# Gate products of an mLSTM layer with the tokens as stationary operand, summed on VectorE and turned back by TensorE

## The reference

```python
h_in = _rmsnorm(x, norm1_w)
q = (h_in @ wq) ; k = (h_in @ wk) ; v = (h_in @ wv)      # 128, 128, 256 columns
o_pre = h_in @ w_og                                      # 256 columns
i_pre = cap(h_in @ w_ig + b_ig)                          # 8 columns, cap(x) = 15 tanh(x / 15)
f_pre = cap(h_in @ w_fg + b_fg)                          # 8 columns
logfg = log_sigmoid(f_pre) ; Fcum = cumsum(logfg)        # along the tokens
Dmat = Fcum[s] - Fcum[t] + i_pre[t], causal ; m = max over t
C = (q k^T / 4) * exp(Dmat - m) ; n = max(|sum C|, exp(-m)) ; h = (C / n) v
```

## Time and profile before

| | |
|---|---|
| median of three executions | 673.02 us |
| profiled execution, its own time | 672.34 us |
| its span, first to last instruction | 670.6 us |
| granted TensorE clock, mean over the span | 0.995 |
| TensorE busy | 658.1 us (98%) |
| VectorE busy | 438.3 us (65%) |
| ScalarE busy | 411.3 us (61%) |
| GpSimd busy | 246.7 us (37%) |

### The profile page before, as it was taken

The page is one execution under the profiler, slowest core; times in us unless marked ns, Lnnn a source line. Parts: engine busy times, 40 slices in busy tenths (PEclk is TensorE's granted clock), DMA queues, the critical chain, the costliest instruction groups (busy, mean ns, idle before and its releaser), DMA issues. The chain is left out here.

```text
span 670.6 us, 15275 instructions
## 1 busy us (share of the span) xinstructions
PE 658.1 (98%) x5297; PEld 633.0 (94%) x5297; DVE 438.3 (65%) x968; ACT 411.3 (61%) x1085; POOL 246.7 (37%) x279
## 2 busy tenths in 40 slices
PE   8999999999999999999999999999999999999995
PEld 8999999999999999999999899999987799999995
DVE  6556557557666655765665576556569986556877
ACT  5556677666776666866577773334689864333553
POOL 3731972134353133632328555112451462222011
PEclk9999999999999999999999999999999899999999
DMA  7174654435534436534363404000166100000000
GB/s 254 37 219 160 193 172 140 133 101 174 168 127 113 127 108 185 161 128 126 97 183 124 111 1 151 32 0 2 48 208 243 65 1 1 1 1 0 1 33 31
DMA packets 38172, 69.74 MB, mean 104 GB/s; under 512 B 3440, under 2 KB 22640, under 8 KB 37872
## 3 DMA queue, kind: packets, MB, share of 16 engines
q1 hardware_dynamic: 37696, 68.38, 32.8%
q10 hardware_dynamic: 432, 0.79, 0.4%
HBM read 52.18 MB, written 16.97 MB: 103 GB/s over the span
## 5 line engine op out<-in xcount | busy, mean ns | idle before, releaser
L312 PE MATMUL PJ<-xTh,WBh 128*128 128x256 f32 x364 | 106.7, 293 | 0.3 <-POOL WBl L839 0.3
L314 PE MATMUL PJ<-xTh,WBl 128*128 128x256 f32 x364 | 103.0, 283 | 0.0
L313 PE MATMUL PJ<-xTl,WBh 128*128 128x256 f32 x364 | 102.8, 283 | 0.0
L824 POOL TENSOR_TENSOR stage<-stage 128x256 f32<-128x256 f32 x32 | 24.5, 766 | 165.0 <-DVE stage L691 165.0
L584 ACT ACTIVATE probs<-probs,rinv 128x256 f32<-128x256 f32 x128 | 58.4, 507 | 26.7 <-DVE rinv L707 26.7
L1202 PE MATMUL UG<-xTh,WBh 128*128 (+1 forms) x256 | 73.6, 288 | 0.3 <-PEq L54 0.3
L1205 PE MATMUL UG<-xTh,WBl 128*128 (+1 forms) x256 | 72.4, 283 | 0.0
L1203 PE MATMUL UG<-xTl,WBh 128*128 (+1 forms) x256 | 72.4, 283 | 0.0
L1274 ACT ACTIVATE ga<-UG 128x256 f32<-128x256 f32 x64 | 24.5, 383 | 75.1 <-PE UG L1205 75.1
L312 PEld LDWEIGHTS PJ<-xTh,WBh 128*128 128x128 f32 x364 | 69.6, 191 | 0.9 <-issue 0.5
L313 PEld LDWEIGHTS PJ<-xTl,WBh 128*128 128x128 f32 x364 | 69.6, 191 | 0.0
(11 more groups left out here) (320 smaller groups left out, 2385.9 us busy)
## 6 DMA issues: line engine op xcount, KB each, us to landing
K<-scr_k SPq DMA_DIRECT2D x60, 256.0 KB, 4.3
raw<-in_w_att SPq DMA_DIRECT2D x37, 256.0 KB, 4.7
Q<-scr_q SPq DMA_DIRECT2D x15, 512.0 KB, 7.5
stage<-scr_m SPq DMA_DIRECT2D x6, 768.0 KB, 5.9
scr_q<-rot_h SPq DMA_DIRECT2D x30, 128.0 KB
scr_q<-rot_l SPq DMA_DIRECT2D x30, 128.0 KB
scr_k<-rot_h SPq DMA_DIRECT2D x30, 128.0 KB
scr_k<-rot_l SPq DMA_DIRECT2D x30, 128.0 KB
```

What stands on the lines that cost most here:

```text
L312: pe.matmul(out, ah, bh, start=(i == 0), stop=False)
L313: pe.matmul(out, ah, bl, start=False, stop=False)
L314: last = pe.matmul(out, al, bh, start=False, stop=(i == n - 1))
L824: pool.tensor_tensor(y[:, 0:S], c[:, 0:S], sn[:, S:2 * S], ALU.subtract).then_inc(rope_sum, 1)
```

## The change

The gate products turn round: 128 tokens are stationary (a tile of `xh_v` or `xl_v`), and 32 weight columns move (8 heads x 2 gates x high and low part). A token tile of a batch takes 4 matmuls, a batch 8, all batches 32. High and low part of the weights give separate columns in OUTS; VectorE adds the pairs with two reduce instructions (`add_gates`) and writes the sums into `gt` with tokens on partitions; TensorE turns them back with 4 transposes into X (`gates_T`); then the Tanh reads X for both gates. `gt` is set to zero at the layer's start. The gates of batches 0, 1 and 2 stand together behind project(0); those of batch 3 come behind q and k of batch 1; `gates_T` stands between the two halves of v and output gate of batch 1. The gate weights are stored without padding. ScalarE's order changes too: it runs `gates` in two parts with half of `evac_og(1)` between them, and the MLP's weight pieces 5 to 11 stand at other places between the evacuations.

```diff
-        WGh, WGl = (gate_w[:, i * 2 * KT * WIDE:(i + 1) * 2 * KT * WIDE].rearrange("p (t g n) -> p t g n", t=KT, g=2)
-                    for i in range(2))
+        WG = WI[:, 11, PIECE - KT * 2 * GATES:].rearrange("p (t l n) -> p t l n", t=KT, l=2)
+        WG_part = [WG[:, :, l, :].rearrange("p t (g h) -> p t g h", g=2) for l in range(2)]
...
-        gate_sums = (X[:, 0:S], OUTS[:, 1, 0:S])
+        gate_parts = OUTS[:, 1, 0:B * TT * 2 * GATES]
+        gate_tok = gt[:, :, :].rearrange("p a s -> p (a s)").rearrange("p (t g k) -> p t g k", t=TT, g=2)
+        gate_sums = (X[:, 0:S], X[:, S:2 * S])
...
-                w = slice(96 - 32 * c, 96 - 32 * c + P)
-                for n, out in enumerate(gate_sums):
-                    for i in range(3 * KT):
-                        t, (a, b) = i // 3, ((WGh, xh_v), (WGh, xl_v), (WGl, xh_v))[i % 3]
-                        last = pe.matmul(out, a[:, t, n, w], b[:, t, c, :], start=(c == 0 and i == 0),
-                                         stop=(c == B - 1 and i == 3 * KT - 1))
-                last.then_inc(s_["gates_ready"], 1)
+                for t in range(TT):
+                    rows, at = slice(t * P, (t + 1) * P), (TT * c + t) * 2 * GATES
+                    for i in range(2 * KT):
+                        last = pe.matmul(gate_parts[:, at:at + 2 * GATES], (xh_v, xl_v)[i % 2][:, i // 2, c, rows],
+                                         WG[:, i // 2, :, :], start=(i == 0), stop=(i == 2 * KT - 1))
+                if c == B - 1:
+                    last.then_inc(s_["gates_ready"], 1)
+
+            def gates_T():
+
+                pe.wait_ge(s_["gates_added"], 2)
+                for n in range(2):
+                    for t in range(TT):
+                        last = pe.transpose(gate_sums[n][:, t * P:(t + 1) * P], gate_tok[:, t, n, :], ident[:, :])
+                last.then_inc(s_["gates_ready"], 1)
...
             project(0)
-            for c in range(B - 2):
+            for c in range(B - 1):
                 project_gates(c)
             pe_T(pe, 1, B - 1)
-            project_gates(B - 2)
-            project_qk(1)
+            project_part(1, 0)
+            project_part(1, 1)
             project_gates(B - 1)
-            project_vog(1)
+            project_vog(1, 0)
+            gates_T()
+            project_vog(1, 1)
             project(2)
...
+            act_hi(act, 1, 3)
             evac_og(0)
-            act_hi(act, 1, 3)
-            mlp_hi(5, 6)
             evac_q(1)
-            mlp_hi(6, 7)
             evac_k(1)
+            mlp_hi(5, 7)
+            gates_tanh()
+            evac_og(1, range(1))
+            gates_log()
+            evac_og(1, range(1, TT))
+            evac_q(2)
             mlp_hi(7, 8)
-            gates()
-            evac_og(1)
-            mlp_hi(8, 9)
-            evac_q(2)
-            mlp_hi(9, 10)
             evac_k(2)
-            mlp_hi(10, 12)
+            mlp_hi(8, 10)
             evac_og(2)
+            mlp_hi(10, 11)
             exp_nm()
+            mlp_hi(11, 12)
...
+            dve.memset(gt[:, :, :], 0.0).then_inc(s_["consts_set"], 1)
...
+            def add_gates():
+
+                dve.wait_ge(s_["gates_ready"], 1)
+                dve.wait_ge(s_["consts_set"], 4)
+                parts = gate_parts.rearrange("p (c t l g h) -> p g c t h l", c=B, t=TT, l=2, g=2)
+                for n in range(2):
+                    out = gate_tok[:, :, n, :].rearrange("p t (c k) -> p c t k", c=B)[:, :, :, 0:HM]
+                    dve.tensor_reduce(out, parts[:, n], axis=AX.X, op=ALU.add).then_inc(s_["gates_added"], 1)
...
-            split(1)
+            split_q(1)
+            add_gates()
+            split_k(1)
+            take_v(1, 0)
+            take_v(1, 1)
             chain()
```

More of the change, by code:

```diff
@@ L936 @@
 WIDE = 96 + P
+GATES = 2 * HM
 def layers(nc, keep, wl_d, wg_d, bg_d, cols_d, mask_d, wm_d, w8_d, sdown_d, out_d):
@@ L1001, in layers @@
         stage1 = sb("stage1", [P, HM * 384])
-        wg_f = stage1[:, 0:2 * KT * WIDE].rearrange("p (t g n) -> p t g n", t=KT, g=2)
+        wg_f = stage1[:, 0:2 * KT * WIDE].rearrange("p (t g n) -> p t g n", t=KT, g=2)[:, :, :, 96:96 + HM]
         A = [a[:, :].rearrange("p (h n) -> p h n", h=HM) for a in (stage, stage1)]
@@ L1017, in layers @@
             xt_ready xt_hi xt_split x_added scaled stored
-            bgs_ready qk_ready qk_hi qk_split vog_ready v_taken og_ready gates_ready gates_tanh sp_ready
+            bgs_ready qk_ready qk_hi qk_split vog_ready v_taken og_ready gates_ready gates_added gates_tanh sp_ready
             chain_step m_ready nm_ready m_out masked_rows rows_ready gcol_ready enm_ready
@@ L1476, in project_gates, with project_part @@
+                if c == B - 1:
[5 more added lines that the diff above has]
+                        last = pe.transpose(gate_sums[n][:, t * P:(t + 1) * P], gate_tok[:, t, n, :], ident[:, :])
                 last.then_inc(s_["gates_ready"], 1)
-            def project_qk(c):
+            def project_part(c, i):
                 if c == 0:
@@ L1481, in project_qk @@
                     pe.wait_ge(s_["wl_split"], LP - 1)
[L1482 to L1497, removed]
+                else:
+                    pe.wait_ge(s_["qk_split"], 2 * c - 1 + i)
@@ new lines, in project_part, with project_vog @@
+                for n in range(2):
+                    w = slice((2 * i + n) * P, (2 * i + n + 1) * P)
+                    last = six(UG[i][:, n * S:(n + 1) * S], [(WLh[:, t, w], WLl[:, t, w]) for t in range(KT)],
+                               x_parts(c))
+                last.then_inc(s_["qk_ready"], 1)
+            def project_vog(c, t):
+                if c:
+                    pe.wait_ge(s_["og_ready"], 2 * (c - 1) + t + 1)
+                rows = slice(t * P, (t + 1) * P)
+                six(UG[2 + t][:, :], [(xh_v[:, f, c, rows], xl_v[:, f, c, rows]) for f in range(KT)],
+                    [(WLh[:, 2 + f, :], WLl[:, 2 + f, :]) for f in range(KT)]).then_inc(s_["vog_ready"], 1)
@@ L1499, in project @@
             def project(c):
-                project_qk(c)
-                project_vog(c)
+                project_part(c, 0)
+                project_part(c, 1)
+                project_vog(c, 0)
+                project_vog(c, 1)
             def rows_T():
@@ L1647, in _ @@
             act.wait_ge(s_["wg_in"], 16)
-            act.activation(WGh, wg_f, ACT.Copy).then_inc(s_["wg_hi"], 1)
+            act.activation(WG_part[0], wg_f, ACT.Copy).then_inc(s_["wg_hi"], 1)
             act.wait_ge(s_["small_in"], 16 * 4)
@@ L1661, in evac_k, with evac_og, gates_tanh @@
                                scale=cols[:, C_SIGN:C_SIGN + 1]).then_inc(s_["qk_hi"], 1)
-            def evac_og(c):
-                for t in range(TT):
+            def evac_og(c, which=range(TT)):
+                for t in which:
                     act.wait_ge(s_["v_taken"], 2 * c + t + 1)
                     act.activation(og_v[:, c, t, :], UG[2 + t][:, D:2 * D], ACT.Tanh, scale=0.5).then_inc(s_["og_ready"], 1)
-            def gates():
-                act.wait_ge(s_["gates_ready"], B)
+            def gates_tanh():
+                act.wait_ge(s_["gates_ready"], 2)
                 act.wait_ge(s_["bgs_ready"], 1)
@@ L1678, in gates, with gates_log @@
                 act.activation(gt[:, 1, :], gt[:, 1, :], ACT.Exp, scale=-CAP).then_inc(s_["gates_tanh"], 1)
+            def gates_log():
                 act.wait_ge(s_["gates_tanh"], 2)
@@ L1823, in _ @@
             dve.wait_ge(s_["wg_hi"], 1)
-            dve.tensor_tensor(WGl, wg_f, WGh.bitcast(F32), ALU.subtract).then_inc(s_["wg_split"], 1)
+            dve.tensor_tensor(WG_part[1], wg_f, WG_part[0].bitcast(F32), ALU.subtract).then_inc(s_["wg_split"], 1)
             dve.wait_ge(s_["small_in"], 64)
             dve.tensor_scalar(bgs[:, :], bg[:, :], 1.0 / CAP, None, ALU.mult).then_inc(s_["bgs_ready"], 1)
+            def add_gates():
+                dve.wait_ge(s_["gates_ready"], 1)
+                dve.wait_ge(s_["consts_set"], 4)
+                parts = gate_parts.rearrange("p (c t l g h) -> p g c t h l", c=B, t=TT, l=2, g=2)
+                for n in range(2):
+                    out = gate_tok[:, :, n, :].rearrange("p t (c k) -> p c t k", c=B)[:, :, :, 0:HM]
+                    dve.tensor_reduce(out, parts[:, n], axis=AX.X, op=ALU.add).then_inc(s_["gates_added"], 1)
             def chain():
```

1 line of the change is left out of this document (removed).

## The result

The change makes the kernel **slower**: four executions took 681.43, 684.46, 685.11 and 686.60 us, against 672.57 us for the kernel before on the same chip (median of four). The ratio is 1.017, 95% interval 1.0149 to 1.0191. Predicted were 671.5 us and a range of 669.8 to 673.4; the result lies outside it, on the side that had 0.09.

A forecast was written before the change was run, and what follows sets the result against it. TensorE was taken to bound the kernel, busy throughout the projections. Saving 1.61 us there, less 0.13 lost at a late mask, gave -1.5 us: 671.5 us from 673.02, range 669.8 to 673.4.

The forecast's parts named there:

- the side that had 0.09: Whole kernel: chance 0.09 that the change is slower, from two clock falls or unhidden weight loads.
- What TensorE saves: Gate matmuls in the projections: 32 at 0.116 us replace 5.76 us; with transposes of 0.44, 1.61 us less.
- Neither bound: Gate matmul pace: from 0.055 us a pair (3.56 us saved) to 0.160 (0.20 saved).
- the rival of unhidden loads: Gate matmuls: each weight load adds to its matmul, 0.47 us a pair, 682.7 us in all; chance 0.04.
- The sums: Two VectorE reduces ahead of `gates_T`: 0.58 us for both, covered by 1.38 us of matmuls, so TensorE waits for nothing.
- the gate path: From project(0) through the gates to the broadcasts: Ln, `chain` and the broadcasts come 0.1 us later than before.
- so it lands at 499.33: Running maximum's first quarter, read back from DRAM: issued at 495.63, takes 3.7 us; 0.8 us of slack before its mask.
- fits with nothing to spare: VectorE before the first weights: masks, split and copies end at 501.96, wanted at 502.02.
- GpSimd's last splits end about 1.4 us later; the MLP needs them 40 us later: GpSimd's splits of MLP weights: the delay was listed among what costs nothing.
- the broadcast rows take the gain: Rival at the masks: a later gate path costs 0.1 us per 0.1; 1 us later gives 672.5 us; chance 0.17.
- The clock rival: TensorE's clock halves at the gates, losing 1.7 us: 673.2 us, or 674.9 with two falls; chance 0.18.
- Against: ... the heads, also short work, mostly keep full clock: Argument against a clock fall at the gates: dense projections ahead, and short work in the heads mostly at full clock.

The follow-up runs named there:

- e13: The change with gates of batches 0 to 2 spread, the instruction fetch moved, and GpSimd's last splits earlier, against the kernel before: 670.78 us, ratio 0.9981.
- e11: The changed kernel itself run once more, nothing edited, against the kernel before: 682.83 us, ratio 1.016.
- e12: The change with gates of batches 0 to 2 spread and 27 passed semaphore tests that move the fetch, against the kernel before: 671.29 us, ratio 0.9983.
- e8: The kernel before without its four dummy matmuls behind the first scores, nothing of the change in it: 684.47 us, ratio 1.0022 to the kernel before.
- e3: The change with four dummy matmuls ahead of the first scores and five instead of four behind them, against the kernel before: 672.86 us, ratio 0.9996.
- e4: The change with ScalarE's old order put back from the Tanh on: 678.83 us, long half-clock falls in 2 of 4 executions.
- e10: The change with 28 passed semaphore tests on TensorE in project(0) and project(1) that move the instruction fetch, against the kernel before: 673.40 us, ratio 0.9999.
- e14: The change with only ScalarE's order edited so that GpSimd's last splits come earlier, against the kernel before: 681.65 us, ratio 1.0107.
- e2: The change with seven dummy matmuls between turning the gate rows and batch 3's projections, against the kernel before: 672.82 us, ratio 1.0004.

## Why the prediction was wrong, point by point

- **What TensorE saves: right.** Predicted 0.116 a pair and -1.61 us; measured 0.111, and -1.69 to the first scores where nothing waits. Neither bound was near, the pace is that of the scores' pairs though a matmul has 32 columns and not 128 or 256, and the rival of unhidden loads is refuted.
- **The sums, and the gate path: right.** Two reduces took 0.49 together (0.58 predicted) and TensorE did not wait for them. Ln came 17.39 us behind the first projection (492.94 - 475.55), before 17.46: 0.1 earlier, where 0.1 later was predicted.
- **"so it lands at 499.33", used for the changed kernel too: failed.** The sum took the way through DRAM over unchanged, and had the first mask wait for nothing past 499.43, 25.67 us behind the first projection; it came at 26.41. The second write landed 2.9 to 3.3 us after its issue instead of 1.6, as the fetch of TensorE's program fell on it; moving only the fetch brought 1.6 back. With twelve matmuls and twelve weight loads fewer ahead of it, the fetch came 20.56 us behind the first projection instead of 19.30. The prediction had counted that VectorE's work "fits with nothing to spare", and so had nothing for this. With fetch and splits out of the way (e13) the first mask did start at 25.67 (499.19 - 473.52).
- **"GpSimd's last splits end about 1.4 us later; the MLP needs them 40 us later": failed.** The lateness was right, the cover was not: with their new place they run into the first mask and cost it 0.34 us (nothing in e11's trace of the same kernel, 1.14 in e12's).
- **A wait priced as its own length: the step that decides.** The rival "the broadcast rows take the gain" had the mechanism and said that each 0.1 us costs 0.1: 672.5 for 1 us. Up to the first scores that held (-1.01 instead of -1.6). But the wait stood where TensorE's clock was nearly lost already (e8), and there the heads took 8.25 us more in the profiled execution, and 12.2 in e8's (49.4 against 37.2). That cost stood nowhere in the sum or in a rival.
- **The clock rival: right mechanism, wrong place and length.** The falls it priced do occur, 3.4 us in the gates in three (e3, e4, e10) of seven profiles with the gates in one block, and cost about the 1.7 it said (29.03 in e10 against 27.47 in e13); with spread gates none of five profiles has one, too few to show that spreading ends them. "Against: ... the heads, also short work, mostly keep full clock" was the error: they kept it by four dummies, a thing that could have been asked of the trace before. Its rows had the signs: a wait of 0.21 at 506.37, shortly behind those dummies, and 3.4 us at half from 520.9.
- **The sum of the parts.** The predicted -1.5 us is what the change gives when both collisions are gone and the gates are spread: -1.67 by medians (670.78 against 672.45), -1.3 by the ratio, interval -2.2 to -0.3. It is no merit of the forecast, whose kernel had none of these edits.

Shown by single edits: the fetch delays the write (e10), the late write brings the long falls (e10 takes both away, e14 keeps both), dummies hold them off (e3, e8), and so does arriving later (e2). Each rests on counts of executions and one profile. Argued only: why an execution that starts late keeps half clock for 24 to 34 us; in the profiles with one, full clock came back in the second half of the heads.

## What to carry to other kernels

A saving on the bounding engine moves everything that is timed against it by accident: instruction fetches, the other engines' last jobs, the places where dummy work holds the clock. Before costing a shorter stage at its own microseconds, list what runs in the shadow of the next handover, and ask what a half-microsecond wait there does to the clock and not only to the time. When a change comes out far off its sum, look for the first wait behind it, and then move one neighbour at a time.

## What the runs showed of the hardware

- A fetch of 16 KB of an engine's program shares the DMA engines with data. Where it began 0.9 us or more ahead of the issue of a write of 64 KB, the write took 1.6 to 1.7 us to its landing (six traces); where it began between 0.3 us ahead and 1.5 us behind, 2.2 to 3.8 us (ten traces). Twelve matmuls and their weight loads fewer were enough to move it there, 28 instructions more to move it off.
- Once the clock was down in this stretch of 32-row and 33-column matmuls, it stayed at half for 23.9, 27.3 or 34.1 us, though TensorE was busy 10.00 of 10.00 us.
- Pairs of a 128-column load and a 32-column matmul go 0.111 us apart at full clock.
- VectorE's mask (two SBUF inputs) and GpSimd's split exclude each other while one of them runs: the mask lost 0.33 to 1.14 us in four traces, the splits 0.45 in one.
